# Two message layers and three linear layers on one core: copied rows awaited by VectorE, far index read a pair ahead

## The reference

```python
def _L0_gnn_ref(x, edge_index, ...):            # 2 message layers
    h = x @ W_enc.T + b_enc
    for l in range(n_layers):
        m = concatenate([h[row], h[col]])
        m = relu(m @ msg_W1[l].T + msg_b1[l])   # one message for each edge
        m = m @ msg_W2[l].T + msg_b2[l]
        agg = segment_sum(m, col)
        upd = concatenate([h, agg]) @ upd_W[l].T + upd_b[l]
        h = _layer_norm(h + upd, ln_g[l], ln_b[l])
    return h @ W_out.T + b_out

def _L1_gnn_ref(x, edge_index, Wl, bl, Wr):     # 3 linear layers
    for i in range(3):
        agg = segment_sum(h[src], dst) * inv_deg
        h = agg @ Wl[i].T + bl[i] + h @ Wr[i].T   # and relu but in the last
    return h
```

## Time and profile before

| | |
|---|---|
| median of 3 runs | 3308.69 us |
| profiled execution | 3326.47 us |
| its span | 3324.7 us |
| TensorE busy (PE / weight loads PEld) | 2891.8 us (87%) / 2669.6 us (80%) |
| VectorE busy | 2279.7 us (69%) |
| ScalarE busy | 1698.9 us (51%) |
| GpSimd busy | 702.0 us (21%) |
| chain that ended last | PE 63%, DVE 12%, DMA 9%, issue 8% |

### The profile page before, as it was taken

How to read it: one execution, slowest core, us unless ns; L and a number is a source line. 1 busy time by engine, 2 the same in 40 slices (tenths; PEclk the granted TensorE clock), 3 DMA queues, 4 the chain that set the end, 5 groups by cost and what they waited for, 6 DMA issues and landing times.

```text
span 3324.7 us, 214437 instructions
## 1 busy us (share of the span) xinstructions
PE 2891.8 (87%) x88629; PEld 2669.6 (80%) x88629; DVE 2279.7 (69%) x4258; ACT 1698.9 (51%) x3386; POOL 702.0 (21%) x934
## 2 busy tenths in 40 slices
PE   4666665799999998799999997689999889998998
PEld 3554554699989987699988887589999889998998
DVE  8999999777767776677767775589999832223211
ACT  1333333677767776777767775668777600001000
POOL 2211123500011115400011114334544500000000
PEclk7777776899999999899999999799999999999999
DMA  3000000566666662466656664045555568876888
GB/s 73 7 6 6 6 6 16 170 185 184 183 165 179 177 176 86 129 183 185 188 165 176 173 175 117 8 160 188 183 184 187 170 215 280 281 250 205 286 278 252
DMA packets 365971, 518.83 MB, mean 156 GB/s; under 512 B 152479, under 2 KB 275909, under 8 KB 365895
## 3 DMA queue, kind: packets, MB, share of 16 engines
q1 hardware_dynamic: 352557, 498.96, 50.0%
q0 software_dynamic: 4000, 8.20, 2.4%
q10 hardware_dynamic: 9338, 10.73, 1.1%
HBM read 408.98 MB, written 108.72 MB: 156 GB/s over the span
## 4 chain that ended last, share of the span: by engine, by line
PE 63%; DVE 12%; DMA 9%; issue 8%; ACT 3%; POOL 2%; SPq 1%; ACTq 0%; DVEq 0%; POOLq 0%
PE psum L1394 19%; PE psum L1618 10%; PE psum L1412 9%; PE psum L1398 9%; PE psum L1605 6%; DMA ovrow<-rows_of_h,ovcur 6%; PE psum L1585 3%; DMA cells_kept<-arena 2%; DMA tabf<-in_x 1%; PE psum L700 1%; DVE Hf L1078 1%; DVE AGGf L984 1%; PE psum L2137 1%; DVE Hf L939 1%; POOL arena L2080 1%
## 5 line engine op out<-in xcount | busy, mean ns | idle before, releaser
L1394 PE MATMUL psum<-tabf,arena 125*32 125x128 f16 x40256 | 1099.6, 220 | 48.5 <-issue 32.3
L1394 PEld LDWEIGHTS psum<-tabf,arena 125*32 125x32 f16 x40256 | 952.0, 97 | 123.3 <-issue 89.0
L1398 PE MATMUL psum<-arena 96*32 96x128 f16 x20928 | 1040.8, 221 | 5.9 <-issue 5.8
L1445 ACT ACTIVATE arena<-psum 128x512 f32<-128x512 f32 x1300 | 776.6, 597 | 369.5 <-PE psum L1398 317.6
L1398 PEld LDWEIGHTS psum<-arena 96*32 96x32 f16 x20928 | 698.4, 95 | 5.6 <-issue 1.8
L1618 PE MATMUL psum<-tabf,arena 125*125 125x256 f16 x5000 | 569.0, 275 | 4.3 <-DVE tabf L2179 4.3
L1412 PE MATMUL psum<-arena 128*32 128x129 f32 x10400 | 565.6, 277 | 0.0
L1618 PEld LDWEIGHTS psum<-tabf,arena 125*125 125x125 f16 x5000 | 557.7, 138 | 5.1 <-issue 5.1
L1645 ACT CAST arena<-psum 125x500 f16<-125x500 f32 x625 | 352.6, 580 | 99.1 <-PE psum L1585 45.4
L1605 PE MATMUL psum<-tabf,arena 125*125 125x256 f16 x2500 | 381.3, 275 | 8.3 <-ACT arena L1645 8.0
L1682 DVE SCALAR_TENSOR_TENSOR acc<-Hf,selfs,psum 125x128 f32<-125x128 f32 x102 | 35.5, 348 | 431.7 <-PE psum L1618 431.5
(11 more groups left out here) (324 smaller groups left out, 4346.0 us busy)
## 6 DMA issues: line engine op xcount, KB each, us to landing
arena<-cells_kept SPq DMA_DIRECT2D x200, 787.5 KB, 5.1
cells_kept<-arena SPq DMA_DIRECT2D x625, 126.0 KB
arena<-slots_turned_from SPq DMA_DIRECT2D x152, 384.0 KB
tabf<-slots_turned_from SPq DMA_DIRECT2D x150, 384.0 KB
arena<-slots_turned_from SPq DMA_DIRECT2D x50, 512.0 KB
tabf<-slots_turned_from SPq DMA_DIRECT2D x50, 512.0 KB
arena<-slots_turned_to SPq DMA_DIRECT2D x152, 96.0 KB
tabf<-slots_turned_to SPq DMA_DIRECT2D x150, 96.0 KB
```

The lines of the kernel that those rows point to most:

```text
L1394: pe.matmul(psCell[b][q:q + GW, g * D:(g + 1) * D], fr, rows, start=g == 0 and p == 0, stop=False, tile_position=(0, q), skip_group_check= ...
L1398: m = pe.matmul(psCell[b][q:q + GW, g * D:(g + 1) * D], toB[part][:, here + q:here + q + GW], cur[:, part, g, :], start=g == 0 and 4 * k + ...
L1445: act.activation(msgs[:, SLOT[pos], :, 0:D], psCell[SLOT[pos]].rearrange("p (c d) -> p c d", d=D), ACT.Relu).then_inc(f_msg, 1)
```

## The change

Six things change.

1. **TensorE's waits in the message layers.** The waits for `f_cur`, for `f_msg` ahead of each gather, and for `f_add` ahead of a half's first scatter are removed from TensorE. VectorE takes two of them over: it waits for `f_cur` of the half ahead of `toB` (line 1464), and for `f_add` of the half ahead of the marks (line 1472). So what raises `f_toN` and `f_toE` implies them. (The message that a gather waited for is one that the scatter issued just ahead of it has waited for already.)
2. **ScalarE's copies.** At a layer's start both halves of the first tile are copied. In the loop the first half's copy stands ahead of the relu of position 2, the second half's ahead of the last relu, both for the next tile. SyncE's loads of `stack_in` wait for a count of copies that fits this.
3. **Cleared rows.** The three memsets of line 1490 are done once, in `first_dve`, and `arena` is divided in another order, so that nothing else writes those rows later. TensorE's wait for `f_one` at a layer's start goes from `4 * (l + 1)` to `4 + l`.
4. **Far index of the message layers.** The copy of the index moves behind the landing of the pair before (`next_index`), into the same buffer; the indirect DMA is issued as soon as the far rows' buffer is free. `ovidx` has one more column, set to 0, for the last, unused copy.
5. **Far index of the linear layers.** The same in all three.
6. **Far product.** In the last two linear layers the far product of a pair's second tile moves from the tile's middle to behind its first matmul.

```diff
         arena_words = 11808
+        STAGE_USED = 2 * 2 * 128 + 3 * 2 * D + 3 * 2 * 2 * D + 3 * 2 * D
...
         toN = [carve([P, n * RG * CELL], F16) for n in SPAN]
+        toE = [carve([128, n, RG, GW]) for n in SPAN]
+        carve([128, STAGE_USED - sum(n * RG * CELL // 2 + n * RG * GW for n in SPAN)])
         toB = [carve([STACKED, n * RG * CELL], F16) for n in SPAN]
-        toE = [carve([128, n, RG, GW]) for n in SPAN]
-        cur = carve([STACKED, 2, RG, D], F16)
         ovrows = carve([128, CP, D], F16)
...
         msgs = carve([128, CELL_RING, RG, W + 1])
+        cur = carve([STACKED, 2, RG, D], F16)
...
                         if half == 0:
-                            stack(1 - w, bass.ds(i * 2 + (w + 1), 1), i * 2 + (1 + tiles_before(kk, False) + w))
+                            stack(1 - w, bass.ds(i * 2 + (w + 1), 1), i * 2 + (2 + tiles_before(kk, True) + w))
...
+            def next_index(t):
+
+                at = slice(t, t + 1) if isinstance(t, int) else bass.ds(t, 1)
+                pool.tensor_copy(ovcur[:, 0:1], ovidx[:, at]).then_inc(f_ovi, 1)
+
             def far_rows(t):
 
-                pool.tensor_copy(ovcur[:, 0:1], ovidx[:, bass.ds(t, 1)]).then_inc(f_ovi, 1)
-                hold(pool, "pool", f_ovi, t + (l * PAIRED + 1))
+                hold(pool, "pool", f_ovi, t + (l * (PAIRED + 1) + 1))
                 pool.indirect_dma_start(ovrows.rearrange("p c d -> p (c d)"), None, far_dram,
...
             with pool.Fori(0, PAIRED) as i:
                 hold(pool, "pool", f_gat, i * (2 * VISIT[1]) + visit_done(-1, kk, VISIT[1] - 1, 2))
                 far_rows(i)
                 pool.wait_ge(f_over, i * 16 + (l * PAIRED + 1) * 16)
                 pool.sem_inc(f_far, 2)
+                next_index(i + 1)
...
                     if at in (0, 3):
 
-                        half = part_of(at)
-                        pe.wait_ge(f_cur[half], i + (tiles_before(kk, half == 0) + tile + 1 + half))
-                        pe.wait_ge(f_toN, i * 2 + part_done(kk, tile, half))
-                    pe.wait_ge(f_msg, before_visit(i, kk, pos))
+                        pe.wait_ge(f_toN, i * 2 + part_done(kk, tile, part_of(at)))
...
                         pe.wait_ge(f_toE, i * 2 + marks_done(kk, 0, half))
-                        pe.wait_ge(f_add[half], i + (kk * (NT + half) + 1 + half))
...
-                pe.wait_ge(f_one, 4 * (l + 1))
+                pe.wait_ge(f_one, 4 + l)
...
                         for pos in range(n):
+                            if pos == 2:
+                                own_rows(0, 1 - w, ..., i * (2 * n) + visit_done(w, kk, 2, 2))
+                            if pos == n - 1:
+                                own_rows(1, 1 - w, None, i * (2 * n) + visit_done(w, kk, n - 1, 2))
                             act.wait_ge(f_gat, i * (2 * n) + visit_done(w, kk, pos, 2))
...
-                            if pos == 0:
-                                own_rows(1, w, None, i * (2 * n) + visit_done(w - 1, kk, n - 1, 2))
-                            if pos == 3:
-                                own_rows(0, 1 - w, ..., i * (2 * n) + visit_done(w, kk, 2, 2))
...
+                    hold(dve, "dve", f_cur[half], i * 2 + (tiles_before(kk, True) + w + tile + 1 + half))
                     dve.tensor_scalar(toB[half][0:CP * GW, span], ...).then_inc(f_toN, 1)
...
+                    dve.wait_ge(f_add[half], i * 2 + (kk * (NT + half) + w + tile + 1 + half))
                     dve.tensor_tensor(toE[half][:, 0:count], ...
...
-                if h == 0:
-                    for unused in (toB[0], cur, toB[1]):
-                        dve.memset(unused[CP * GW:STACKED], 0.0).then_inc(f_one, 1)
...
             def far_rows(i):
 
+                hold(pool, "pool", l_ovi, i + (l * (PAIRED + 1) + 1))
                 hold(pool, "pool", l_ovd[1], i + (l * PAIRED + 1))
-                pool.tensor_copy(ovcur[:, 0:1], ovidx[:, bass.ds(i, 1)]).then_inc(l_ovi, 1)
-                hold(pool, "pool", l_ovi, i + (l * PAIRED + 1))
                 pool.indirect_dma_start(ovrow[:], None, rows_dram, ...
...
+                hold(pool, "pool", l_ovr, i * 16 + 16 * (l * PAIRED + 1))
+                next_index(i + 1)
...
-                if first + KEPT == NT:
+                if u == 0 and first + KEPT == NT:
                     far_total(i, u)
                 for k in range(KEPT):
+                    if u == 1 and first + k == 1:
+                        far_total(i, u)
...
         def first_dve(dve):
             dve.wait_ge(s_pset, CONSTANTS + L0 + 2)
             dve.tensor_copy(AGG[:, :, D], selfs[0:P, 1:NT + 1])
+            dve.wait_ge(o_ST, SORTS)
+            for u in range(2):
+                dve.wait_ge(o_store[u], 32 * (SORTS // 2 + 1))
+            for unused in (toB[0], toB[1], cur):
+                dve.memset(unused[CP * GW:STACKED], 0.0).then_inc(f_one, 1)
             dve.wait_ge(s_norms, 3)
```

More of the change, by code:

```diff
@@ L234, in build @@
         colg = sb("colg", [128, 126], BF16)
-        ovidx = sb("ovidx", [128, PAIRED], I32)
+        ovidx = sb("ovidx", [128, PAIRED + 1], I32)
         ovto = sb("ovto", [128, NT])
@@ L1248, in cells_sp @@
                     for w in range(2):
[L1249 removed]
+                        stack(w, slice(w, w + 1), 1 + tiles_before(2 * l, True))
             sp.wait_ge(f_stack[1], 32 * (l + 1))
@@ L1283, in cells_sp @@
                     if half == 0:
-                        stack(1, slice(NT - 1, NT), 1 + tiles_before(kk, False) + NT - 2)
+                        stack(1, slice(NT - 1, NT), 1 + tiles_before(kk, True) + NT - 1)
                 if h == 0:
@@ L1357, in cells_pool @@
             kk = 2 * l + 1
+            if l:
+                hold(pool, "pool", f_ovi, l * (PAIRED + 1))
+            next_index(0)
             hold(pool, "pool", f_table, 32 * NB_LOOPS * (l + 1))
@@ L1434, in cells_act @@
             act.wait_ge(m_low, (l + 1) * DUOS)
-            own_rows(0, 0, 32 * (l * (NT + 1) + 1), visit_base(2 * l) + ahead(2 * l, 2))
+            for half in range(2):
+                own_rows(half, 0, 32 * (l * (NT + 1) + 1), visit_base(2 * l) + ahead(2 * l, 2))
             for h in range(2):
@@ L1564, in linear_pool @@
                 own_slots(slice(0, 1), 0)
+            hold(pool, "pool", l_ovi if l else f_ovi, (l if l else L0) * (PAIRED + 1))
+            next_index(0)
             hold(pool, "pool", h_rows, 32 * NB_LOOPS * (l + 1))
@@ L2348, in _ @@
             pool.sem_inc(l_chunk, KEPT_BUFFERS)
+            pool.memset(ovidx[:, PAIRED:PAIRED + 1], 0)
             pool.memset(to_slots[:, :, NT, :], 0.0).then_inc(f_pad, 1)
```

14 lines of the change are left out of this document (8 added, 6 removed).

## The result

| | before | after |
|---|---|---|
| median, 4 runs each on one chip | 3309.27 us | 3285.69 us |
| ratio of the runs | | 0.9929, 95% interval 0.9912 to 0.9946 |
| profiled execution | 3326.47 us | 3281.49 us |

The change makes the kernel faster, by 23.6 us (18 to 29), where 66.6 was forecast and 3277 was the upper end of the range. The kernels of e1, e4 and e8 reach the same point at 584.1, 584.3 and 582.6 (586.3 before, 578.8 after), so it moves by several us from one execution to the next. So I compare stretches, not ends.

What follows compares the result with a forecast made beforehand. The prediction took TensorE as the bound, with idles for instruction issue and, in the last linear layers, waits for far rows. Terms 5.6 + 22 + 0 + 35 + 4 = 66.6 off 3308.7 gave 3242 us, range 3214 to 3277.

Steps and rivals of the forecast that it cites:

- Start of a layer: Message layers' start: without the three memsets TensorE's first matmul comes 2.8 us earlier, twice, 5.6 us.
- TensorE's waits: Message loops: removing met waits saves instructions, 0.14 a tile in the first stage, 0.10 in the others, 22 us.
- VectorE's waits: Message loops: the waits VectorE takes over make its tile 5.24 us, beside TensorE's 5.57, at no cost.
- ScalarE and SyncE: Message loops: the moved copy of 0.60 stays hidden by 0.6, row loads are asked for earlier, nothing is later.
- Far index in the message layers: Indirect DMA starts some 0.7 us earlier, but TensorE hardly waits for its landing: gain 0.
- Linear layers 2 and 3: Last two linear layers: a lead of 3.0 us a pair covers the waits for far rows, 35 us.
- First linear layer: GpSimd issues its DMA and own-slot copies earlier; most comes back as another wait, 4 us.
- TensorE's stop at each far DMA: Seven-visit message stages: the stop of 0.9 us a pair moves with the DMA's issue and stays, gain 0.
- rival 4: Message loops: VectorE's second one-hot waits for late copied rows and sets the pace, 6.44 a tile, 3359 us; chance 0.06.

Runs made afterwards that it cites:

- e1: Changed kernel, but SyncE asks for a tile's rows one tile earlier in the message layers; ratio to before 0.9872, 3271.17 us.
- e4: Kernel before with only the linear layers' two edits (far index a pair ahead, far product moved); ratio to before 0.9908, 3283.70 us.
- e8: Kernel before with only the far product's move in the last two linear layers; ratio to before 0.9924, 3283.99 us.
- e5: e1 with TensorE's removed waits put back beside VectorE's; ratio to before 0.9943, 3291.21 us.
- e9: e1, with SyncE holding one list load a pair until the far rows have landed, in the seven-visit stages; ratio to before 0.9765, 3241.12 us.
- e3: e1 with the message layers' far index copied in line as before; ratio to before 0.9870, 3269.59 us.
- e10: e9 with the message layers' far index copied in line as before; ratio to before 0.9797, 3249.60 us.
- e7: Changed kernel with ScalarE's copies in their old places, behind the relus of positions 0 and 3, and counts to fit; ratio to before 1.0270, 3400.30 us.
- e12: Changed kernel, with SyncE holding the list load of the pair's other tile until the far rows have landed; ratio to before 1.0375, 3432.21 us.
- e2: Changed kernel with the message layers' far index copied in line, as before; ratio to before 0.9975, 3305.69 us.
- e6: e1, but SyncE asks for a tile's rows behind the lists of both halves; ratio to before 0.9896, 3276.85 us.
- e11: Changed kernel with only the list hold of e9, rows asked for as late as in the changed kernel; ratio to before 0.9932, 3291.19 us.

## Why the prediction was wrong, step by step

- **Start of a layer: right.** TensorE's idle ahead of its first matmul fell from 8.28 to 5.62 and from 7.78 to 5.08, 2.7 each (2.8 forecast). The memsets fitted with 0.39 us to spare. The second one-hot came 0.24 later than without the new wait, not 0.1.
- **TensorE's waits: right.** 22 forecast, 23 measured by e5 against e1 (13 to 34), 19.5 in the loops.
- **VectorE's waits: right that they fit beside TensorE, wrong in one half of the sum.** The marks start 0.42 to 0.53 behind the start of the sum (0.44 forecast, 0.20 in the earlier trace rows). But the copied rows hold nothing where they are in time: in the first stage of e1 the second one-hot starts 0.53 behind the first in all 97 halves, as before, not 0.70. VectorE's wait for TensorE there is 15.2 us in 26 pieces, one of them 3.8, where the prediction had one in each half. The stretch by the rule of the Trainium skill (VectorE: DVE Perf Modes, The DRAIN you can't avoid), no extra cost of the semaphore, isn't what the trace shows: about 0.25 more; that the same section lets an operation that isn't held start earlier fits the 0.20.
- **ScalarE and SyncE: the step that failed.** "The row loads on SyncE are asked for earlier by the count that they wait for, so nothing is later there." The count was read as earlier, but it had become that of the copy of the next tile: later by a tile, against a copy placed earlier. Price: 19 us (e1; 21 in the loops).
- **Far index in the message layers: failed too.** "TensorE hardly waits for its landing, so no gain" took the landing as fixed. There was 6.5 - 5.7 = 0.8 us of room. The list load that ScalarE's late copy had held back moved ahead of the transfer, and the landing came 0.7 later in the mean, 1.2 in the median. Price on top of the first: 35 us between e1 and e9 (0.9872 to 0.9765; 24 to 46), 26 in the loops (17 with the index in line, between e3 with 1241.3 and e10).
- **Linear layers 2 and 3: right.** 35 forecast; 35.3 in the traces, 30 (23 to 38) on the chip by e4.
- **First linear layer: small in the changed kernel's trace, nearly right over all.** 4 forecast, 427.2 us before and 426.5 after (between the first and the last pair's far product). VectorE's wait for GpSimd's copies did fall, from 17.2 to 10.4 us, and TensorE's load unit then waited 12.6 us for VectorE's one-hots instead of 17.6, but 16.1 for ScalarE's counts instead of 11.2: most came back as another wait. But this trace is the slowest of the twelve with the edit, which run from 422.0 to 426.5 with a mean of 423.8; the two without it have 427.2 and, in e8, 426.6. So the edit gives about 3.

So of the forecast 66.6 the start of the layers (5.4) and the late linear layers came. TensorE's waits came too, but were lost again in the message loops, which should have given 22 and cost 10: 32 of the 43 missing us. About 3 are the first linear layer as it stands in this trace and 5 the late linear layers, which gave 30 on the chip for 35 in the traces; the rest is within the uncertainty of the difference, 6. With both causes taken out (e9) the gain is 78 us, about 11 more than the forecast: the prediction took TensorE's stop at each far DMA as unchanged, and in e9 it is 0.34 us a pair shorter, 17 us. In the changed kernel itself it is unchanged: the load unit's idles of over 0.1 us beside the issue are 0.81 us a pair, 0.82 before, 0.48 in e9.

The range failed because each of the two steps was priced at nothing, with no bound for what it could cost. None of the rivals was a late load: rival 4 put the danger on VectorE, which e7 shows to be real but which this order avoids.

## What to carry to other kernels

- When a copy, a wait or a count moves, write down for each load when it is asked for and when it is needed, in tiles, before and after; a count that is one higher is a tile of lead lost.
- A wait on the queue engine also spaces the loads behind it. When it goes or is met earlier, look which transfer with little room (here 0.8 us) now stands behind them, and hold the loads that have time; e12 shows what it costs to hold one that has none.
- Removing waits that are met is a gain on the engine that sets the end (here 23 us, some 0.12 a tile); moving them costs nothing where the other engine has room.

## What the runs showed of the hardware

- A GpSimd indirect DMA takes 1.0 to 1.3 us to issue, and up to 2.15 while VectorE's one-hot from uint8 to fp16 (1.0 to 1.3 us) runs; it goes with the time shared (correlation 0.86 over 50). A small copy on GpSimd takes 0.58 us beside VectorE's one-hot in fp16, and 0.18 without.
- TensorE's stop at this issue is 0.92 us a pair at an issue of 1.21, and 0.58 at 2.0 (e1, e9): it doesn't grow with the issue. Nor is it the early start alone that shortens it: in e7 the issue starts as early and takes 1.2, and the load unit's idles beside it are 0.80 us (0.82 before, 0.48 in e9). What makes the stop stays open.
- The same far rows take 2.7 us from the end of their issue to the landing when no list load is asked for until then (e9, e10, e12), 2.7 to 3.0 when one is asked for 0.6 to 1.6 behind that end (before, e4, e7, e8), and 3.7 to 4.2 when one is asked for ahead of it, by the median (changed, e1, e2, e3, e5, e6, e11). The delay lies ahead of their first packet, not in the packets.
